# Cross-attention in a decoder layer: the next batch's value products move from groups 5 and 6 to groups 6 and 7

## The reference

```python
v = (values @ Wv.T).reshape(N, -1, HEADS, HEAD_DIM)      # 16 heads of 16
k = (keys @ Wk.T).reshape(N, -1, HEADS, HEAD_DIM)
q = (query @ Wq.T).reshape(N, -1, HEADS, HEAD_DIM)
energy = jnp.einsum('nqhd,nkhd->nhqk', q, k)
attn = jax.nn.softmax(energy / HEAD_DIM ** 0.5, axis=-1)
out = jnp.einsum('nhqk,nkhd->nqhd', attn, v).reshape(N, Q, EMBED)
return out @ Wo.T + bo
```

## Time and profile before

| | |
|---|---|
| median of three executions | 1164.34 us |
| profiled execution, its own time | 1168.91 us |
| its span in the trace | 1166.8 us |
| PE busy over the span | 1009.4 us (87%) |
| DVE busy | 808.7 us (69%) |
| ACT busy | 756.4 us (65%) |
| POOL busy | 628.8 us (54%) |
| attention, first turned group to last | about 753 to 929 us from the span's start |

### The profile page before, as it was taken

The page is one execution under the profiler, slowest core; times in us unless marked ns, Lnnn a source line. Parts: engine busy times, 40 slices in busy tenths (PEclk is TensorE's granted clock), DMA queues, the critical chain, the costliest instruction groups (busy, mean ns, idle before and its releaser), DMA issues.

```text
span 1166.8 us, 16801 instructions
## 1 busy us (share of the span) xinstructions
PE 1009.4 (87%) x5808; PEld 691.1 (59%) x5808; DVE 808.7 (69%) x954; ACT 756.4 (65%) x1727; POOL 628.8 (54%) x389
## 2 busy tenths in 40 slices
PE   5795788988889898888988898898989799799995
PEld 3342554555555455554555566677767556699994
DVE  6786999998999989999899945756666721111110
ACT  4789998888989888898888911455565532133331
POOL 2000899898999989899899933421210005022222
PEclk9897799999999999999999999979998979899998
DMA  5001333343444433343444401430000006689994
GB/s 180 8 7 36 87 108 108 98 109 91 116 110 96 117 96 103 107 106 105 102 109 106 107 22 62 131 93 15 14 2 2 2 0 220 216 257 321 300 319 113
DMA packets 91119, 125.45 MB, mean 108 GB/s; under 512 B 11641, under 2 KB 84490, under 8 KB 91018
## 3 DMA queue, kind: packets, MB, share of 16 engines
q1 hardware_dynamic: 87130, 120.04, 35.8%
q0 software_dynamic: 3904, 4.33, 2.0%
HBM read 115.93 MB, written 9.23 MB: 107 GB/s over the span
## 4 chain that ended last, share of the span: by engine, by line
PE 37%; DVE 26%; issue 12%; DMA 11%; POOL 6%; ACT 6%; DVEq 0%; POOLq 0%; ACTq 0%
DVE states L1681 14%; PE ps L1186 12%; DMA sums<-y_tile,x_tile 10%; DVE states L1659 5%; PE ps L1077 4%; PE ps L1067 3%; PE ps L1167 3%; POOL states L663 3%; PE ps L1279 3%; PE ps L1291 2%; POOL states L672 2%; PE ps L1084 2%; DVE neg_max L1762 2%; PE ps L1177 2%; ACT probs L989 2%
## 5 line engine op out<-in xcount | busy, mean ns | idle before, releaser
L672 POOL TENSOR_TENSOR states<-states,c_row 128x800 f32<-128x800 f32 x255 | 473.9, 1889 | 131.8 <-DVE states L1681 131.8
L1186 PE MATMUL ps<-states,ident 128*128 128x400 f32 x1024 | 370.7, 506 | 0.0
L1186 PEld LDWEIGHTS ps<-states,ident 128*128 128x128 f32 x1024 | 188.2, 193 | 119.2 <-issue 7.5
L1681 DVE TENSOR_TENSOR_SCAN states<-ps,states 128x800 f32<-128x800 f32 x128 | 230.5, 1801 | 12.4 <-POOL states L663 12.4
L1681 DVE TENSOR_TENSOR_SCAN states<-sb_decay,ps 128x800 f32<-128x800 f32 x128 | 231.4, 1808 | 10.7 <-ACT sb_decay L901 10.6
L893 ACT ACTIVATE xT<-xn_tok,xT 100x256 f32<-100x256 f32 x512 | 216.4, 493 | 14.8 <-PE ps L1167 14.7
L901 ACT ACTIVATE ps<-dt,neg_a 128x396 f32<-128x396 f32 x256 | 141.8, 586 | 57.9 <-DVE states L1681 56.9
L1167 PE MATMUL ps<-ident,xT 100*128 100x100 f32 x1024 | 113.9, 255 | 73.1 <-DVE states L1681 70.9
L1167 PEld LDWEIGHTS ps<-ident,xT 100*128 100x128 f32 x1024 | 97.9, 144 | 131.6 <-issue 127.0
L901 ACT ACTIVATE sb_decay<-dt,neg_a 128x396 f32<-128x396 f32 x256 | 144.4, 612 | 2.4 <-DVE states L1681 2.4
L1048 ACT ACTIVATE hid_tile<-ps,w_tile 128x128 f32<-128x128 f32 x160 | 45.6, 368 | 105.0 <-PE ps L1490 105.0
(11 more groups left out here) (225 smaller groups left out, 1270.1 us busy)
## 6 DMA issues: line engine op xcount, KB each, us to landing
c_row<-rows SPq DMA_DIRECT2D x256, 200.0 KB, 3.1
w_tile<-in_w SPq DMA_DIRECT2D x40, 1024.0 KB, 7.9
b_row<-rows SPq DMA_DIRECT2D x32, 200.0 KB, 3.1
ctx<-in_ctxT SPq DMA_DIRECT2D x8, 361.0 KB, 4.1
rows_by_slot<-blank_rows SPq DMA_DIRECT2D x1, 2660.0 KB, 11.5
x_tile<-rows_by_slot SPq DMA_DIRECT2D x20, 133.0 KB, 3.7
win<-in_winT SPq DMA_DIRECT2D x2, 1024.0 KB, 10.8
w_shared<-in_w SPq DMA_DIRECT2D x2, 1024.0 KB, 6.6
```

The lines of the kernel that those rows point to most:

```text
L672: nc.gpsimd.tensor_tensor(st, st, c_row[i % C_SLOTS][:].unsqueeze(1).broadcast_to([P, CP, TQ]), ALU.mult).then_inc(product_ready, 1)
L1186: mm = nc.tensor.matmul(ps[:, j, 0:TQ], ident[:], states[i % RING][:, j * TQ:(j + 1) * TQ], start=False, stop=(i % N == N - 1), skip_group ...
L1681: nc.vector.tensor_tensor_scan(st, rates, inflows, 0.0, ALU.mult, ALU.add).then_inc(scan_done, 1)
```

## The change

One constant. The two parts of the next batch's `values` (PE) and of `copy_values` (DVE) run in groups 6 and 7, and group 5 has neither:

```diff
-MASS_AT, PROJECT_AT, KEYS_AT, VALUES_AT = 1, 2, (3, 4), (5, 6)
+MASS_AT, PROJECT_AT, KEYS_AT, VALUES_AT = 1, 2, (3, 4), (6, 7)
```

## The result

The changed kernel takes 1171.42 us (median of six runs, 1169.04 to 1172.55) against 1163.8 us for the kernel before (median of six, 1160.28 to 1166.03). The ratio is 1.0065, with a 95% interval of 1.0047 to 1.0084: slower by 7.6 us. The profiled execution took 1171.77 us with a span of 1169.6 us. The one of before took 1168.91 us, 5 us over its own median, so the two traces are compared by stretches and not by their spans.

The account below looks back on a forecast made before the run. It took TensorE as nearly full (19.29 of 21.40 us a batch), the loop hanging on VectorE's chain. Hold 1.5 plus clock 4.8 made 6.3 us, stated as 1170.3 us; range 1163.0 to 1179.0, the forecast's own 1166.8 to 1175 us.

Parts of the forecast that it names:

- The wait moves and grows: TensorE's 0.90 us wait before the first values becomes 1.32 us before group 6's transposes, which need VectorE's probability copy.
- The hold: VectorE's two small inv_rows copies stand behind GpSimd's split: 0.36 us a batch more, 1.5 us for five batches.
- Rival 2: Second inv_rows copy also waits for GpSimd's second instruction, ctx_l: 9.6 us in place of 1.5; chance 0.16.
- The clock: TensorE's granted clock falls to 1.2 GHz behind the new wait in four of six batches, 1.2 us each: 4.8 us.
- the old falls: Clock drops in the first groups of batches 3 and 5 before the change, 5.3 us in the trace.
- The sum: Whole kernel: 1.5 + 4.8 = 6.3 us longer; profiled execution about 1175.2 us, median 1170.3 us.
- Rival 1: The wait moves to group 6 but the clock stays; only the hold costs, 1165.8 us; chance 0.27.
- Rival 3: The old falls vanish and the new wait brings none: 5.3 us back, 1.5 us lost, 1160.5 us; chance 0.10.

Follow-up runs that it names:

- Experiment 9: Changed kernel with the late split, ScalarE and VectorE taking the second half of the keys in group 5 instead of 4: 1152.24 us, ratio 0.9896.
- experiment 4: Changed kernel with eight products, result unused, put into TensorE's 1.3 us wait of group 6: 1170.81 us, ratio 1.0048.
- the late split: GpSimd's context split also waits for VectorE's small inv_rows copies of the same batch; put into the changed kernel: 1173.24 us, ratio 1.0063.
- experiment 7: Changed kernel with VectorE copying the last values before the reciprocal and inv_rows copies in group 7: 1171.83 us, ratio 1.0063.
- experiments 4 to 6: Experiment 4, experiment 6 and, between them, the changed kernel with eight unused products and the late split: 1159.41 us, ratio 0.9953.
- experiment 3: Kernel before the change, with the late split added: 1158.72 us, ratio 0.9948.
- experiment 1: Changed kernel with only the second part of the values moved (groups 5 and 7), the first left behind the keys: 1164.6 us, ratio 0.9995.
- experiment 10: Changed kernel with the second half of the keys taken in group 5, without the late split: 1151.48 us, ratio 0.991.
- experiment 8: Values in groups 5 and 7, with the late split: 1152.69 us, ratio 0.9899.
- experiment 6: Changed kernel with the late split and four unused products, instead of eight, in the 1.3 us wait: 1155.63 us, ratio 0.9943.

## Why the prediction held, point by point

**The wait moves and grows.** Worked out: from 0.90 before the values to 1.32 us before `turn_probs(6)`. Measured: 1.32 to 1.34 us, six times. Experiment 9 bears out the cause that was named, `copy_probs(5)` behind `low_keys`: with their order changed (and ACT's part of the keys moved too) the wait is 0.38 us.

**The hold.** Worked out: POOL 0.18 us ahead of the small copies, both of them through before `ctx_l`, `copy_probs` 0.36 us later. Measured: 0.19 us ahead, both past GpSimd's first instruction and not held by its second in five of five, 0.39 us a batch (experiment 4). Rival 2, the second copy caught as well, did not happen once.

**The clock.** Worked out: falls behind the new wait in about four of six batches, 1.2 us each. Measured in the one trace: four (batches 1, 2, 3 and 5), 1.5 to 1.6 us each (23.29, 23.33, 23.34 and 23.40 less 21.79). That it was just four is luck: the count was a guess, and the same wait brought six falls of six with the late split. The size was a little low: the 0.66 us wait that follows is as long as without a fall, so it took nothing in. The prediction let the old falls stand. In the trace two (1.57 and 3.72 us) went, and one of the old kind came, in the first groups of batch 4 (24.92 - 21.79 = 3.13 us). The reason given for the fall was in part misread: full-size products stand only behind the 0.90 us wait; ahead of it stand transposes and scores, as ahead of the new one. What differs is what comes after the wait, and its length, and no run separates the two.

**The sum.** By the stretches: falls 9.33 us now less 5.29 us before, hold 5 x 0.39 = 1.95 us, last stretch -0.11 us: 5.88 us, against 139.01 - 133.19 = 5.82 us measured. This closes by its making, since a fall is counted as what a stretch has above 21.79 us, and 21.79 is 21.40 + 0.39. The forecast's 6.3 us is near to it in part by luck: the new falls cost 6.2 us and not 4.8, the hold less the last stretch 1.84 us and not 1.5, and the old falls, left as they were in the sum, changed by -2.2 us and made up for it. The time forecast for the profiled execution, 1175.2 us, came out 3.4 us too long (1171.77 us), because the rest of the span was 3.0 us shorter. The medians say 7.6 us against the 6.0 us stated, inside the forecast's own range; the stretches of these two traces account for 5.8 of them, and the execution of the kernel before that was traced took longer than any of its timed ones. That the falls in the timed runs are those of the trace is not shown; the mean granted clock on record for them goes the same way, 0.943 to 0.946 in the six of the changed kernel, and 0.945 to 0.957, with a median of 0.947, in 25 of the kernel before.

**Rival 1**, the clock stays, fell: it went down behind the open wait four times in six, in experiment 7 three times in five and, with the late split, six in six; with the wait filled (experiments 4 to 6) or its cause removed (9 and 10) never. **Rival 3**, the old falls vanish and nothing new comes, is what experiment 3 made of the kernel before, but not what the change did.

What stays open is how many falls a timed execution has, why the same wait brings a fall in one batch and none in the next, and why the lower clock lasts 3.4 us behind the wait in one kernel and 6.8 us in another.

## What to carry to other kernels

A wait that is dodged by moving the waiting work goes to the next instruction in the queue. If that one depends on the same engine's queue, as `turn_probs(6)` on a copy behind `low_keys`, nothing is gained, and the new wait may be in a worse place. Look at the order on the engine that is late before you move the work that waits for it: here the move alone cost 0.65%, and with the order changed as well the kernel is 1% faster than before. And where two engines share a resource, look at what the moved work releases: here GpSimd's start moved, so that its first instruction and not its second held VectorE's copies, and one more wait on GpSimd, which had nothing to hurry for, was worth 0.5% in the kernel before.

## What the runs showed of the hardware

- A small SBUF-to-SBUF copy on VectorE (100x128, 0.22 us alone) takes up to 1.36 us when GpSimd's product has started first, and ends 0.08 us after it. Of two in a row the second then starts as GpSimd's product ends (801.98) and takes 0.21 us; GpSimd's next instruction starts at 802.06, while the record of that copy runs to 802.20, and neither is stretched (1.59 us for GpSimd's). The Trainium skill, "SBUF — State Buffer", section "SBUF: two separate sides", says that the one that starts first holds the shared ports for its whole instruction; the trace agrees for the held copy.
- TensorE's granted clock went to its lower level (1.2 GHz) after single waits of 1.32 us among transposes, scores and small products: four times in six in the changed kernel, six in six with the late split. It also went there where waits of about 0.67 and 0.41 us lay 2.4 us apart, in two of five batches of the kernel before and of experiment 4, one of five in the changed kernel and in experiment 1, and none of five in experiment 10; and in two of five in experiment 7, where they were 0.33 and 0.41 us. It did not after 0.90 us alone (none of six batches, experiment 8) or 0.65 us alone (none of six, experiment 6). So in these traces the lengths of the waits alone do not say whether a fall comes.
- About half a microsecond of products whose result nobody reads (experiment 6) was worth 3 us a batch (20.75 against 23.72 to 23.77 us, both with the late split), which I had not expected.
